# Two rests a tile from VectorE to GpSimd, with a longer ring and fewer gathers at a time

## The reference

```
e = stack([tbl_f[ids[:, f]] for f in range(39)], axis=1)   # 1024 x 39 x 16
x0 = xk = e
for W, b in ((w0, b0), (w1, b1), (w2, b2)):                # 39 x (39 or 64) x 128
    z = relu(einsum('bhd,bkd,hks->bsd', x0, xk, W) + b)
    # layers 0 and 1: z[:, :64] is the next xk, z[:, 64:] goes out; layer 2: all of z goes out
z = sum over d of concat(all that went out)                # 1024 x 256
h = relu([z, dense_ctx] @ W_top1 + b_top1)                 # 512
h = relu(h @ W_top2 + b_top2)                              # 256
y = h @ W_top3                                             # 1024 x 1
```

## Time and profile before

| | |
|---|---|
| median of three runs | 1394.54 us (1391.05 to 1398.18) |
| the profiled execution | 1390.81 us |
| its span in the trace | 1389.0 us |
| mean granted TensorE clock | 0.984 of full speed |

### The profile page before, as it was taken

How to read it: one execution, slowest core, us unless ns; L and a number is a source line. 1 busy time by engine, 2 the same in 40 slices (tenths; PEclk the granted TensorE clock), 3 DMA queues, 4 the chain that set the end, 5 groups by cost and what they waited for, 6 DMA issues and landing times.

```text
span 1389.0 us, 15495 instructions
## 1 busy us (share of the span) xinstructions
PE 1241.1 (89%) x4128; PEld 769.5 (55%) x4128; DVE 1164.8 (84%) x1054; ACT 653.5 (47%) x757; POOL 909.8 (66%) x581
## 2 busy tenths in 40 slices
PE   0148999997999999999999999999999999999989
PEld 0014666564665666565665666565655666665643
DVE  1128899997999999999999999999999999999950
ACT  1114454553545465555545454555454454454522
POOL 6726877774777777777777677676777754555520
PEclk9969999998999999999999999999999999999999
DMA  7297777788677778877777778888777777778500
GB/s 176 37 193 171 184 176 198 192 206 167 124 181 180 192 184 203 205 180 173 168 185 172 195 178 194 195 205 193 168 170 166 190 187 193 175 194 200 122 0 0
DMA packets 134718, 235.17 MB, mean 169 GB/s; under 512 B 15929, under 2 KB 23082, under 8 KB 134587
## 3 DMA queue, kind: packets, MB, share of 16 engines
q1 hardware_dynamic: 81191, 148.45, 46.2%
q10 hardware_dynamic: 43522, 83.90, 23.2%
q0 software_dynamic: 9984, 2.58, 2.5%
HBM read 231.01 MB, written 6.23 MB: 171 GB/s over the span
## 4 chain that ended last, share of the span: by engine, by line
PE 37%; DVE 22%; POOL 18%; issue 14%; DMA 4%; ACT 3%; DVEq 1%; SPq 0%; ACTq 0%; POOLq 0%
PE z_even L706 20%; POOL gathered L410 13%; PE z_odd L706 12%; DVE whole L616 10%; POOL rest L422 6%; DVE rest L623 4%; DVE whole_psum L616 4%; DVE part L651 2%; ACT head L507 2%; PE whole_psum L784 2%; DMA x_rep<-x_rows 2%; DMA x_shift<-x_rows 1%; DVE sum L649 1%; PE z_even L713 1%; PE x_odd L733 1%
## 5 line engine op out<-in xcount | busy, mean ns | idle before, releaser
L422 POOL TENSOR_TENSOR rest<-whole,head 128x1024 fp32r<-128x1024 f32 x256 | 608.9, 2393 | 325.0 <-ACT head L507 324.6
L616 DVE TENSOR_TENSOR whole<-x_bank,x_rep 128x1024 f32<-128x1024 f32 x448 | 535.3, 1216 | 68.5 <-ACT x_bank L482 62.0
L410 POOL DMA_INDIRECT gathered<-in_tbl,idx x312 | 299.0, 958 | 103.1 <-issue 100.3
L507 ACT CAST head<-whole_psum 128x1024 fp32r<-128x1024 f32 x192 | 194.6, 1013 | 348.6 <-DVE whole_psum L616 340.4
L507 ACT CAST head<-whole 128x1024 fp32r<-128x1024 f32 x256 | 268.6, 1049 | 54.0 <-DVE whole L616 25.2
L623 DVE TENSOR_TENSOR rest<-whole_psum,head 128x1024 fp32r<-128x1024 f32 x192 | 234.6, 1222 | 21.2 <-ACT head L507 21.1
L616 DVE TENSOR_TENSOR whole_psum<-x_bank,x_rep 128x1024 f32<-128x1024 f32 x192 | 235.7, 1227 | 12.4 <-DMA x_rep<-x_rows 10.0
L706 PE MATMUL z_odd<-head,w_rest 128*128 128x512 f32 x460 | 205.8, 447 | 27.2 <-POOL rest L422 23.1
L706 PE MATMUL z_even<-head,w_rest 128*128 128x512 f32 x436 | 194.2, 445 | 24.8 <-DVE rest L623 14.7
L706 PE MATMUL z_odd<-whole,w_whole 128*128 128x512 f32 x400 | 188.8, 602 | 7.3 <-DVE whole L616 7.3
L706 PE MATMUL z_odd<-rest,w_head 128*128 128x512 f32 x460 | 181.0, 393 | 0.0
(11 more groups left out here) (66 smaller groups left out, 895.1 us busy)
## 6 DMA issues: line engine op xcount, KB each, us to landing
x_rep<-x_rows ACTq DMA_DIRECT2D x160, 512.0 KB, 10.7
x_rep<-x_rows SPq DMA_DIRECT2D x160, 512.0 KB, 10.5
x_shift<-x_rows SPq DMA_DIRECT2D x96, 546.0 KB
gathered<-in_tbl,idx POOLq DMA_INDIRECT x312, 7.3
x_rows<-xt SPq DMA_DIRECT2D x32, 78.0 KB
x_rows<-xt SPq DMA_DIRECT2D x32, 40.0 KB
x_rep<-in_W_top SPq DMA_DIRECT2D x2, 512.0 KB, 11.8
w_k<-in_L_rec_w SPq DMA_DIRECT2D x1, 760.5 KB
```

What stands on the lines that cost most here:

```text
L410: nc.gpsimd.indirect_dma_start(gathered[:, f, :], None, tables[f], bass.IndirectOffsetOnAxis(ap=idx[:, f:f + 1], axis=0)).then_inc(s_gathe ...
L422: nc.gpsimd.tensor_tensor(rest[:, split_slot(product)], whole_slot(product), head[:, split_slot(product)].bitcast(F32), ALU.subtract).then ...
L507: nc.scalar.copy(head[:, split_slot(product)], src).then_inc(s_head, 1)
L616: nc.vector.tensor_tensor(out[0:rows, 0:width, :], xk[0:rows, :].unsqueeze(1).to_broadcast([rows, width, N]), x0, ALU.mult).then_inc(s_pro ...
```

## The change

`KINDS` of layer 1 goes from `UVPPUPVPVP` to `UPPPUPVPVP` and of layer 2 from `UUVUPUVPVP` to `UUPUPUVPVP`: pair 1 of layer 1 and pair 2 of layer 2 become P. A tile then has 10 P, 4 V and 6 U pairs, where it had 8, 6 and 6. The ring `whole` gets 8 slots. `GATHERS_BETWEEN` goes from 11 to 7. `ctx_t` moves to partitions 64 to 79 of a buffer that it shares with `xt`, and the weights `wt1c` that are multiplied with it move to the same partitions.

```diff
--- before.py
+++ after.py
@@ -29,11 +29,11 @@
 
 
 
-KINDS = {1: "UVPPUPVPVP", 0: "UUUU", 2: "UUVUPUVPVP"}
+KINDS = {1: "UPPPUPVPVP", 0: "UUUU", 2: "UUPUPUVPVP"}
 ORDER = (1, 0, 2)
-WHOLE_SLOTS = 6
+WHOLE_SLOTS = 8
 SPLIT_SLOTS = 4
-GATHERS_BETWEEN = 11
+GATHERS_BETWEEN = 7
 HEADS_IN_1 = 3
 HEADS_IN_2 = 1
 TRANSPOSES_AFTER = 2
@@ -122,13 +122,14 @@
         bias_t2 = sb("bias_t2", [P, M2])
         wt3 = sb("wt3", [P, M2])
         ctx_rows = sb("ctx_rows", [P, BLOCKS, CTX])
-        ctx_t = sb("ctx_t", [CTX, B])
 
         idx_all = sb("idx_all", [P, BLOCKS, FIELDS], I32)
         idx = sb("idx", [P, FIELDS], I32)
         gathered = sb("gathered", [P, FIELDS, DIM])
         emb = sb("emb", [P, SPC, FIELDS * DIM])
-        xt = sb("xt", [FIELDS, 2, N])
+        xt_and_ctx = sb("xt_and_ctx", [HALF + CTX, 2, N])
+        xt = xt_and_ctx[0:FIELDS]
+        ctx_t = xt_and_ctx[HALF:HALF + CTX].rearrange("p a n -> p (a n)")
         x_shift = sb("x_shift", [ROWS0, CHUNKS0, N])
 
         x_rep = sb("x_rep", [P, LOADS + TWICE, CPL, N])
@@ -151,12 +152,12 @@
         flat = x_rep[:].rearrange("p g c n -> p (g c n)")
         at = [0]
 
-        def in_x_rep(rows, size):
+        def in_x_rep(rows, size, first=0):
             at[0] += size
-            return flat[0:rows, at[0] - size:at[0]]
+            return flat[first:first + rows, at[0] - size:at[0]]
 
         wt1 = in_x_rep(P, 2 * T1).rearrange("p (c m) -> p c m", c=2)
-        wt1c = in_x_rep(CTX, T1)
+        wt1c = in_x_rep(CTX, T1, HALF)
         wt2 = in_x_rep(P, M1 * T2).rearrange("p (c m) -> p c m", c=M1)
         assert at[0] <= TWICE * CPL * N
         h1 = in_x_rep(P, M1 * B).rearrange("p (m n) -> p m n", m=M1)
```

## The result

The changed kernel takes 1398.91 us (median of 20 runs, 1396.59 to 1402.95), the kernel before 1394.9 us in runs beside it (1390.85 to 1398.18). The ratio is 1.0031, 95% interval 1.0022 to 1.0041: 4 us slower, where I forecast 1374. The difference is small, but its interval excludes 1, and the gain of some 20 us is missing.

What follows compares the result with a forecast made beforehand. All three engines nearly full, GpSimd fullest: steady tiles -21.5, last tiles -4, first tiles +2, standstill +1.5, together -22; 4 taken off gives -18, 1372.8, said as 1374 us. Likeliest case 1363 to 1386, wider 1358 to 1394.

Steps and rivals of the forecast that it cites:

- VectorE and GpSimd get in each other's way: Rival, chance 0.03: SBUF accesses of VectorE and GpSimd exclude each other; judged not to block VectorE's products and rests.
- add 0.45: Long stretch, layer 2: the reduction's longer form, a partial sum and an addition, delays pair 2's rest by 0.45 us.
- The first two tiles: +2: First two tiles, 13 gathers each: GpSimd's 40.2 us of work exceeds the stretches of before, costing 2 us.
- GpSimd's load: Steady part, four tiles: rests 95.7, gathers 48.8 and some 3 more make 147.5 us, against TensorE's about 146.4.
- the steady part: Four tiles: long stretches 38.1 and 38.5, two short of 36.7, refill 0.5: 150.5 us against 154.09.
- e + 9.4: Short stretch: TensorE wants layer 2's pair 2 9.4 us after e, when TensorE has finished layer 1 and relus start.
- pair 2 behind the reduction: Long stretch, layer 2: pair 2's product follows VectorE's reduction, its rest ready 10.35 us after TensorE finishes layer 1.
- The signs that I had named: Changed profile: rests x128 and x320, VectorE 79%, GpSimd near 77%, head waits under 8 us, x_bank 2.5 or more per tile.
- sign of being wrong: TensorE waiting over 5 us in four tiles for GpSimd's rests, or short stretches growing beyond 37.1 us.
- GpSimd's standstill: GpSimd stands still once for 10.07 us amid gathers; with a full GpSimd this costs 1.5 us more.
- No cost for the ring, the layout and the x_rep loads: Ring of 8, new rows and x_rep loads cost nothing; no VectorE wait for a ring slot stood in the trace.
- Seven gathers: Short stretch: seven gathers hold GpSimd 8.6 us; pair 2's rest is ready 8.8 us after TensorE finishes layer 1.

Runs made afterwards that it cites:

- e1: Changed kernel, with the addition of the two partial sums reading its first operand from PSUM instead of SBUF: 1381.51 us, ratio 0.9926 to the kernel before.
- e2: Changed kernel, with the addition of layer 2's partial sum moved behind the products of layer 0: 1381.36 us, ratio 0.9921 to the kernel before.
- e3: Changed kernel, with 31 second-block gathers instead of 13 before the first rest, and 4 instead of 13 per early tile: 1385.15 us, ratio 0.9952.
- e6: Kernel before, with the two repairs of e2 and e3 and nothing of the change: 1383.43 us, ratio 0.9956.
- e9: e5 with the reduction of layer 2 after pair 2 in place of pair 1: 1386.06 us, ratio 0.9970 to the kernel before.
- e7: Kernel before, with only the ring of 8 and the new rows of ctx_t and its weights: 1392.46 us, ratio 1.0004.
- e8: e5 with each x_rep load inside the loop bringing 256 of 512 columns: 1373.37 us, ratio 0.9867 to the kernel before.
- e4: Changed kernel, with all gathers between layers 1 and 2 again (GATHERS_BETWEEN 11 in place of 7): 1490.48 us, ratio 1.0713 to the kernel before.
- e10: e5 with the reduction of layer 2 after pair 3 in place of pair 1: 1374.44 us, ratio 0.9879 to the kernel before.
- e5: Changed kernel, with both repairs, those of e2 and e3: 1373.08 us, ratio 0.9874 to the kernel before.

## Why the prediction was wrong

**The step that failed** is the last rival, "VectorE and GpSimd get in each other's way". I checked the rule of the Trainium skill against VectorE's products and rests, which have one input in PSUM, and concluded that nothing is blocked. One instruction of VectorE has both inputs in SBUF, the addition, and I had priced it at its undisturbed length, inside the "add 0.45" of the longer reduction. Beside a rest it takes 2.50 us and not 0.29. That costs 2.2 us in each group of four tiles and 15 us in the run (e1, e2), most of the gain that I forecast. I had also looked only at the durations of GpSimd's rests, which do not change; it is VectorE's instruction that gets longer. The trace of before had the sign, in its timeline of VectorE:

```profile
561.12 0.29 DVE L654 TENSOR_TENSOR sum<-sum,part 128x128 f32 x1
...
582.92 0.61 DVE L654 TENSOR_TENSOR sum<-sum,part 128x128 f32 x1
```

The same instruction has two durations there. The second ran into the end of a rest (GpSimd's two from 578.64 take 4.74, to 583.38) and ended 0.15 us after it. By filling GpSimd's queue in layer 1, the change made this meeting last a whole rest.

**"The first two tiles: +2"** was the second failure: a term of the sum that was too small. The first four stretches together take 158.9 us in the changed kernel and 149.3 before, 9.7 more; 2.7 of it lies in the first, whose length varies by several us from run to run (33.3 to 39.9). I added up GpSimd's load and looked at the landing of gathers only for the steady part. In the first tiles four gathers go behind rests and two more behind layer 2, and `emb` waits for the last of them. With the first tiles put right, the run gets 11 us shorter (e3). About 3 us of this could be had before the change as well: in e6 the second to fourth stretches take 112.8 us, before 115.95. How the rest divides between the late landing and GpSimd's fuller queue is not shown.

**The steady part** was otherwise nearly right. With the addition out of the way four tiles are 151.2 us (e2) for 150.5 reckoned, with long stretches of 38.3 and 38.65 (38.1, 38.5). The short ones are 36.94 and 36.96 in the changed kernel itself, 0.25 over the 36.7. There I misread when TensorE wants pair 2: e + 9.4 was the modelled end of the matmuls ahead of it, but in the short stretch of before TensorE starts the pair 3.03 us after those matmuls start, at e + 8.84. The first two lines are of before, the others of the changed kernel, whose e is 604.76:

```profile
601.63 3.60 PE L706 MATMUL z_odd<-whole,w_whole 128*128 128x512 f32 x8
604.66 0.80 PE L706 MATMUL z_odd<-head,w_rest 128*128 128x512 f32 x1
...
610.57 3.60 PE L707 MATMUL z_odd<-whole,w_whole 128*128 128x512 f32 x8
611.62 2.38 POOL L423 TENSOR_TENSOR rest<-whole,head 128x1024 fp32r<-128x1024 f32 x1
614.06 0.50 PE L707 MATMUL z_odd<-head,w_rest 128*128 128x512 f32 x1
```

The rest is ready at 614.00, e + 9.2 (I had e + 8.8), and TensorE starts 0.06 us later and 3.49 us after the matmuls ahead: it loses 0.46 us that the profile shows as no wait. The reason that I gave for the long stretches, pair 2 behind the reduction, was only half of it (e9): without that wait GpSimd's full queue takes its place.

**GpSimd's load** was put too high, 147.5 us in four tiles. The trace has 132.3 us busy and 8.9 us of gaps before gathers, 141.2 together, while TensorE is busy for 148.7. So GpSimd is not the fullest engine; its times of delivery, not its load, set TensorE back.

**The signs that I had named.** The counts of rests came as said (x128 and x320), and so did VectorE's share of 79%; GpSimd's is 76%, where I had near 77%. GpSimd waits 10.0 us for heads in four tiles, not under 8, and VectorE at most 1.7 us a tile for `x_bank`, not 2.5 or more (3.2 us in four tiles, 6.9 with two waits that the profile ascribes to nothing). Neither sign of being wrong was met: TensorE waits 3.9 us for GpSimd's rests in four tiles, not over 5, and the short stretches stay under 37.1. Both looked at TensorE and GpSimd, and the loss was in an instruction of VectorE.

**GpSimd's standstill.** For the first, of 10 us, I set +1.5; that tile takes 47.5 us for 48.5 before in the profiled executions, so it was no loss. But there is a second, of 3.2 us, in both kernels, at the same count of gathers. Before, GpSimd's spare time hid it (39.31 us for 39.27 elsewhere); now the stretch is 41.40 in place of 38.3.

**No cost for the ring, the layout and the x_rep loads:** right (e7, e8).

**Seven gathers:** right in direction, and far more important than I had it (e4).

In all: 22 us of gain reckoned; 15 taken by the addition, about 7 more than I set by the first tiles, 3 by the second standstill, 4 by the short stretches, and 1.5 given back by the first standstill. That makes a loss of 5 to 6 us. By the profiled executions it is 8.9, by the medians 4. (My 1374 also took only 1 of the 3.7 us by which the median lay above the profiled execution; by my own sum it should have been 1376.5.)

## What to carry to other kernels

Before work is moved to GpSimd, list every VectorE instruction that reads two operands from SBUF, also the smallest: here such an addition, started beside a rest on GpSimd, lasted until the rest had ended (up to 2.53 us for 0.29), and the profile calls it busy. An instruction of one shape with two durations in the trace is a hint of such a meeting; look at what GpSimd does beside it. What helped here was to put it where GpSimd issues gathers (e2), or one operand in PSUM (e1). Read from the trace when an engine starts its next instruction, not when the modelled end of the last one is. And when a queue gets full, look at the first and last tiles by themselves, since their load is another one and their due times are too.

## What the runs showed of the hardware

- A VectorE addition of 128 columns: 0.29 us with one input in PSUM beside GpSimd's rests (e1); 0.28 with two in SBUF beside gathers (e2); 0.61 (before), 2.50 (after), 2.35 (e9) and 1.25 us (e10) with two in SBUF beside a rest, each time to about 0.15 us after the end of that rest. GpSimd's rest itself stays at 2.36 to 2.41 us.
- GpSimd's queue stands still twice amid gathers, for 9.2 to 10.2 and for 3.1 to 3.3 us, in all twelve traces, each time with 113 and 226 gathers ahead of them. What it is stays open.
- The first layer 1 started between 91.6 and 103.1 us in the profiles, with the weight split at 36 to 51 us, and not along with the change: e5 has it at 36, as before.
